# Attention block of a transformer layer on 8 cores: the first key, query, value and output-weight loads issued from the value-transpose stage instead of the attention stage

## What is computed

```python
x = x + attn(layernorm(x), Wq, Wk, Wv, Wo)
x = x + ffn(layernorm(x), W0, bias0, W1, bias1)   # 2048 -> 8192 -> 2048, gelu

def attn(x, Wq, Wk, Wv, Wo):
    q, k, v = x @ Wq.T, x @ Wk.T, x @ Wv.T         # split in 16 heads
    q, k = rope(q), rope(k)
    kw, vw = [previous block, own block] of k, v   # blocks of 512 rows
    scores = q @ kw.T / sqrt(128), masked to j > i and j <= i + 512
    return (softmax(scores) @ vw) @ Wo.T
```

## Time and profile before

| what | us |
|---|---|
| the two timed executions | 3869.8 and 4254.2 |
| their median | 4062.0 |
| the profiled execution's own time | 3853.5 |
| its span (first to last instruction, core 7) | 3851.9 |
| spans of the 8 cores | 3837.4 to 3851.9 |
| mean granted TensorE clock of the cores | 0.937 to 0.943 of full |

### The profile page before, as it was taken

One profiled execution on the slowest core, in us unless ns is written; L12 is line 12 of the kernel. 1 busy time (PEld: TensorE's weight loads), 2 busy tenths in 40 slices (PEclk: granted clock), 3 DMA queues, 4 the chain that ended last, 5 costly groups with the idle time before them and its releaser, 6 DMA issues. The chain is left out here.

```text
span 3851.9 us, 47166 instructions; the slowest of 8 cores (3837.4 to 3851.9 us)
## 1 busy us (share of the span) xinstructions
PE 3273.1 (85%) x17600; PEld 1632.0 (42%) x17600; DVE 785.8 (20%) x1618; ACT 786.3 (20%) x1285; POOL 592.9 (15%) x933
## 2 busy tenths in 40 slices
PE   1599999997357576676749999999997999999999
PEld 1344444443244453535434444444443444444444
DVE  5555554000034444434320000000000000000000
ACT  3355554111332332414101111111110000000000
POOL 1000101001300000000010000001203433443321
PEclk9999999999589888888959999999998999999999
DMA  9322555542774224060262333332807989899764
GB/s 239 100 62 62 99 103 102 100 96 71 256 138 146 74 75 145 1 218 2 82 162 69 82 82 82 82 82 58 150 39 184 225 209 221 212 223 224 198 196 124
DMA packets 191858, 488.96 MB, mean 127 GB/s; under 512 B 21776, under 2 KB 54544, under 8 KB 188816
## 3 DMA queue, kind: packets, MB, share of 16 engines
q0 software_dynamic: 132304, 304.97, 37.6%
q1 hardware_dynamic: 59328, 180.97, 14.2%
HBM read 487.96 MB, written 115.34 MB: 157 GB/s over the span
## 5 line engine op out<-in xcount | busy, mean ns | idle before, releaser
L1186 PE MATMUL pool<-w1q,gq 128*128 128x512 bf16 x4096 | 899.4, 380 | 35.2 <-DMA gq<-g_sp 35.2
L1041 PE MATMUL pool<-ln2T,w0b 128*128 128x512 bf16 x4096 | 886.4, 380 | 2.0 <-PEq L120 2.0
L370 PE MATMUL pool<-ln1T,wbuf 128*128 128x512 bf16 x3584 | 777.0, 380 | 6.6 <-PE pool L370 4.6
L1186 PEld LDWEIGHTS pool<-w1q,gq 128*128 128x128 bf16 x4096 | 396.6, 98 | 521.7 <-issue 55.9
L1041 PEld LDWEIGHTS pool<-ln2T,w0b 128*128 128x128 bf16 x4096 | 401.2, 98 | 487.0 <-issue 5.3
L370 PEld LDWEIGHTS pool<-ln1T,wbuf 128*128 128x128 bf16 x3584 | 350.4, 98 | 433.0 <-issue 13.5
L144 DVE TENSOR_TENSOR obuf<-pool,yh 128x512 f32<-128x512 f32 x64 | 44.3, 691 | 1795.2 <-PE pool L1190 1695.7
L1117 POOL DMA_DIRECT2D gq<-g_sp x256 | 225.4, 900 | 749.1 <-PE pool L1190 558.4
L170 ACT ACTIVATE gst<-pool,bias_s 128x2048 bf16<-128x2048 f32 x64 | 125.9, 1967 | 745.1 <-PE pool L1041 745.1
L785 PE MATMUL pool<-wo_sb,outT 128*128 128x512 bf16 x1024 | 237.0, 394 | 33.3 <-DVE ybuf L889 29.3
L814 ACT ACTIVATE expb<-pool 128x640 bf16<-128x640 f32 x256 | 180.1, 705 | 277.9 <-PE pool L728 271.9
(11 more groups left out here) (59 smaller groups left out, 1927.5 us busy)
## 6 DMA issues: line engine op xcount, KB each, us to landing
gq<-g_sp POOLq DMA_DIRECT2D x256, 512.0 KB, 12.1
w0b<-w_t POOLq DMA_DIRECT2D x128, 256.0 KB, 16.3
g_sp<-gst SPq DMA_DIRECT2D x64, 512.0 KB, 2.6
w1q<-w_t POOLq DMA_DIRECT2D x256, 128.0 KB, 19.3
xb<-x_ctx SPq DMA_DIRECT2D x20, 1024.0 KB, 11.1
wbuf<-wk_t POOLq DMA_DIRECT2D x64, 256.0 KB, 15.1
wbuf<-wv_t POOLq DMA_DIRECT2D x64, 256.0 KB, 14.9
xh<-x_ctx SPq DMA_DIRECT2D x32, 512.0 KB, 5.7
```

The lines of the kernel that those rows point to most:

```text
L370: ins = tn.matmul(pool[:, slot * 2048 + k * 512: slot * 2048 + (k + 1) * 512], lhs, ln1T[:, roff: roff + 512], start=(i == 0), stop=(i == ...
L1041: ins = tn.matmul(pool[:, slot * 2048 + scv * 512: slot * 2048 + (scv + 1) * 512], lhs, ln2T[:, i * TOWN + scv * 512: i * TOWN + (scv + 1) ...
L1186: tn.matmul(pp, lhs, w1q[hq4 % 2][:, n * 512: (n + 1) * 512], start=(n == 0), stop=False)
```

## The change

The five tensors kring, vring, qring, wo_sb and msk get their SBUF space before the value-transpose stage and keep it through the attention stage. The first query block's loads of k and q, the mask and the output weights are issued from within the value-transpose stage, behind the second group of vtl loads; the first loads of v follow behind the fifth group, after a wait for the first 8 tiles of v_sp (4 on each of SP's two write semaphores). In the attention stage POOL's first work is the loads of query block 1. Within a query block the order is now k, q, v (before: k, v, q). Nothing else is changed.

```diff
+        def ring_kq(g, qb):
+            for o0 in range(0, 16, 4):
+                g.dma_start(
+                    kring[:, o0 * 1024:(o0 + 4) * 1024].rearrange(
+                        "p (o c) -> p o c", c=1024),
+                    k_spv[:, o0: o0 + 4, qb * 512: qb * 512 + 1024]
+                ).then_inc(sem["sRing"], 16)
+            for o0 in range(0, 16, 8):
+                g.dma_start(
+                    qring[:, o0 * 512:(o0 + 8) * 512].rearrange(
+                        "p (o c) -> p o c", c=512),
+                    q_spv[:, o0: o0 + 8, qb * 512:(qb + 1) * 512]
+                ).then_inc(sem["sRing"], 16)
+
+        def ring_v(g, qb):
+            for j0 in range(0, 8, 2):
+                g.dma_start(
+                    vring[:, j0 * 2048:(j0 + 2) * 2048].rearrange(
+                        "p (j f) -> p j f", f=2048),
+                    v_spv[:, qb * 4 + j0: qb * 4 + j0 + 2, :]
+                ).then_inc(sem["sRing"], 16)
+
+        def wo_msk_load(g):
+            g.dma_start(msk[:], msk_in).then_inc(sem["sMsk"], 16)
+            for i0 in range(0, 16, 4):
+                g.dma_start(
+                    wo_sb[:, i0 * 2048:(i0 + 4) * 2048].rearrange(
+                        "p (i f) -> p i f", f=2048),
+                    wo_tv[:, i0: i0 + 4, :]
+                ).then_inc(sem["sWo2"], 16)
+
...
                                     vT_sp[o * 128:(o + 1) * 128,
                                           sg4 * 512:(sg4 + 1) * 512]
                                 ).then_inc(vs, 16)
+                            if sg4 == 1:
+                                wo_msk_load(g)
+                                ring_kq(g, 0)
+                        g.wait_ge(sem["sSpVa"], 16 * 4)
+                        g.wait_ge(sem["sSpVb"], 16 * 4)
+                        ring_v(g, 0)
...
                 def _(g):
                     barrier(g)
-                    g.dma_start(msk[:], msk_in).then_inc(sem["sMsk"], 16)
...
-                    rings(0)
-                    for i0 in range(0, 16, 4):
-                        g.dma_start(
-                            wo_sb[:, i0 * 2048:(i0 + 4) * 2048].rearrange(
-                                "p (i f) -> p i f", f=2048),
-                            wo_tv[:, i0: i0 + 4, :]
-                        ).then_inc(sem["sWo2"], 16)
                     for qb in range(1, NQB):
                         g.wait_ge(sem["sQbPE"], qb)
-                        rings(qb)
+                        ring_kq(g, qb)
+                        ring_v(g, qb)
```

More of the change, by code:

```diff
@@ L503, in _ @@
                         s.wait_ge(sem["sSpQb"], 16 * (NP1_G // 2))
+        p2o = ExitStack()
+        kring = p2o.enter_context(nc.sbuf_tensor("kring", [128, 16 * 1024], BF16))
+        vring = p2o.enter_context(nc.sbuf_tensor("vring", [128, 8 * 2048], BF16))
+        qring = p2o.enter_context(nc.sbuf_tensor("qring", [128, 16 * 512], BF16))
+        wo_sb = p2o.enter_context(nc.sbuf_tensor("wo_sb", [128, 16 * 2048], BF16))
+        msk = p2o.enter_context(nc.sbuf_tensor("msk_s", [128, 5 * 640], BF16))
+        k_spv = k_sp.rearrange("(o p) t -> p o t", p=128)
+        v_spv = v_sp.rearrange("(s p) f -> p s f", p=128)
+        q_spv = q_sp.rearrange("(o p) t -> p o t", p=128)
+        wo_tv = wo_t.rearrange("(i p) f -> p i f", p=128)
+        def ring_kq(g, qb):
[26 more added lines that the diff above has]
+                ).then_inc(sem["sWo2"], 16)
         if DO_V:
@@ L585, in build_nc @@
         with p2:
[L586 to L590, removed]
             expb = [p2.enter_context(nc.sbuf_tensor(f"expb{j}", [128, 640], BF16))
@@ L658, in _ @@
                     barrier(g)
-                    g.dma_start(msk[:], msk_in).then_inc(sem["sMsk"], 16)
[L661 to L667, removed]
-                            g.dma_start(
[L669 to L685, removed]
-                    rings(0)
-                    for i0 in range(0, 16, 4):
-                        g.dma_start(
-                            wo_sb[:, i0 * 2048:(i0 + 4) * 2048].rearrange(
-                                "p (i f) -> p i f", f=2048),
-                            wo_tv[:, i0: i0 + 4, :]
-                        ).then_inc(sem["sWo2"], 16)
+                    if not DO_V:
+                        wo_msk_load(g)
+                        ring_kq(g, 0)
+                        ring_v(g, 0)
                     for qb in range(1, NQB):
                         g.wait_ge(sem["sQbPE"], qb)
-                        rings(qb)
+                        ring_kq(g, qb)
+                        ring_v(g, qb)
                 @blk.tensor
@@ L915, in _ @@
                             v.sig(sem["sNmr"])
+        p2o.close()
         if MAX_PHASE < 3:
```

## The result

The changed kernel is slower by 1.15%: the ratio to the kernel before is 1.0115, with a 95% interval of 1.0086 to 1.0145. On the 3870 us of the kernel before that is some +44 us (33 to 56). By a bound of 2% the two are the same. Forecast were +33 us, a ratio of 1.0086. The profiled execution took 3906.5 us, and the lowest of 11 timed ones 3900.6, against 3853.5 and 3845.1 of before. The median of all eleven, 4091.0, lies outside my range, since executions of both kernels fall in two groups several per cent apart, whatever the kernel, and the comparison uses the faster group alone.

A forecast was written before the change was run, and what follows sets the result against it. DMA, not TensorE, was taken to limit the value-transpose stage and first attention loads. Terms -41.7 (ring wait), +73 (eleven loads), +0 (rest of stage), +2 (v loads) gave +33 on 3853.5, or 3886.5 us; range 3862 to 3925.

The forecast's parts named there:

- the rest of the stage: Value transposes from tile 8 to the barrier: pace stays at 49 us, +0; bounds 25 us less, 23 us more.
- the eleven loads: Mask, output weights, k and q queued ahead of the third vtl group make tile 8 of the transposes later: +73 us.
- The ring wait that goes: Start of attention: k, q, v and mask land before the barrier, so TensorE's load wait disappears: -41.7 us.
- starved-writes rival: Value-transpose stage: SP's v_sp writes slow beside POOL's full queue; +64 us in all, 3917.5 us; chance 0.16.
- The v loads at the stage's end: vring's loads, issued after the wait for 8 v_sp tiles, land about at the barrier: +2 us remaining wait.
- Sum: Whole kernel: -41.7 + 73 + 2 = +33 us, giving 3886.5 us; chance 0.64.
- The base and the range: Whole kernel: counted from the profiled execution's 3853.5 us, with a range from 3862 to 3925 us.
- The second way: Before the first score: all DMA time needed, 158 us from about 946, ends at 1104, or +28 us.
- Clock: Transposes: clock at half before and after, and attention starts from there either way: 0 us.
- absorbed: Value-transpose stage: free DMA time takes the moved loads, stage keeps 89 us, ring wait goes; 3811.8 us; chance 0.08.
- Interleaved: Value-transpose stage: vtl loads served beside wo_sb, tile 8 under 73 us late, DMA total rules; +28, 3881.5 us; chance 0.12.
- an estimate of +11: Alternative sum from the skill's HBM share: wo_sb read as f32, some 50 MB, 140 us; set aside for the rows' rates.

The follow-up runs named there:

- e2_wo_only: Changed kernel with only mask and output weights moved early; first k, q and v loads back behind the barrier; profiled execution 3899.4 us, no ratio taken.
- e1: Changed kernel with the four output-weight loads last in POOL's queue of the value-transpose stage, behind the v loads; ratio 1.0117 to the kernel before.
- e3: Changed kernel with the output weights behind the fifth vtl group, ahead of the v loads; profiled execution 3941.6 us, no ratio taken.
- e4: Changed kernel with all moved loads behind the fifth vtl group, in the order mask, k, q, v, output weights; ratio 1.0089 to the kernel before.
- e6_late_wo_after: As e4, but the output weights are issued behind the barrier, as before the change; ratio 0.9973 to the kernel before.
- e8: As e4, but two of the four output-weight loads are issued behind the barrier; profiled execution 3927.5 us, no ratio taken.

## Why the prediction was right and where it was wrong

The mechanism was right: the moved output weights hold up the third vtl group. Two steps failed. The sum came out 8 us too small, for the most part by the +0 for the rest of the stage (measured +5.4) and by +73 for the eleven loads (+76.8). And the range of the total time left no room for how far single executions lie apart. By step:

- *The ring wait that goes, -41.7:* right. It is 42.2 by the medians (1032.9 to 1075.1) and under 1 us after.
- *Eleven loads ahead of the third vtl group, +73:* right in mechanism and nearly in size. Tile 8 is late by 76.8 us (985.3 to 1062.1). Its parts stand up on their own: without the output weights tile 8 came at 1010 (1007 worked out), with them alone at 1043 (1038), and undoing their part gave back 51.7 us where 50.8 were charged.
- *The rest of the stage, +0:* this is the term of the sum that failed most. From tile 8 to the barrier it takes 53.0 us instead of 47.6, +5.4. I had written that the pace stays. From tile 8 on, SP's writes land in 5.6 us where they took 3.1, and ScalarE waits for them 24.5 us instead of 19.3 (medians over the cores). Of the 51.1 and 30.3 us that it waits in the whole stage, the larger part of the difference lies ahead of tile 8, where TensorE waited for the third group anyway. So a part of the starved-writes rival was real, 5 of its 23 us. That the loads queued beside the writes are the cause is supported by the other orders: from tile 8 to the last transpose it takes 46 to 57 us in all the kernels that have more than vtl loads queued there, 40.4 before, and 33.5 in e2_wo_only, where the writes land in 2.8 us. No run changed the queue and nothing else.
- *The v loads at the stage's end, +2:* nothing. On core 4 they were in by 1103.2, ahead of the barrier at 1113.9.
- *Sum:* -42 + 77 + 5 + 0 = +40, where I had +33. The interval of the ratio, 33 to 56, has my value at its edge.
- *The base and the range:* I counted from one profiled execution, 3853.5, and put only half of its distance of 16 us to the lower timed one into the range. That holds for executions like it: the profiled one took 3906.5. But the two timed ones of the kernel before lay 384 us apart, I had seen that, and gave the range no room for it. The median of all timed ones is 4091.0, 166 us above the range's end of 3925. What the runs show instead is a spread of 3900.6 to 4391.6, as wide as that of the kernel before, 3845.1 to 4335.4.
- *The second way, all DMA time together:* it gave 1104, or +28, and was the more general one. Four orders of the same loads (the changed kernel, e1, e3, e4) have their first score within 1.4 us of each other, at 1115 to 1116. Its reason was incomplete: I took it that nobody waits for the output weights once they are issued late enough. By my own steps e4_all_late should have won 14 us, and it lost 41. The wait at the block's end for POOL's loads wasn't in my account at all. In the changed kernel it costs nothing: on core 4 POOL's drain ends at 1105.8, and SP's wait for its last write only at 1113.5.
- *Clock, 0:* not as I wrote. On core 4 the granted clock is 0.87 from 1061 to 1075, right behind the long wait, so mostly at the upper of its two levels, and 0.50, the lower one, from there to 1113; the 16 transposes of a tile take 1.05 us at the one and 1.86 at the other. It shows in no mark, since ScalarE and the writes set the pace.
- *Two small slips:* in slice 11 the DMA digit is 7, not 7 to 9, and the eleven issues add up to 8.3 us in the rows, not 8.4. Nothing hangs on either.
- *The rivals:* absorbed was wrong, since the stage grew by 79 us. Interleaved was wrong too. SP's writes starving was right to a quarter. The HBM share of about 358 GB/s that the Trainium skill states ("DMA: Bandwidth & Descriptors", section "Where 436 GB/s comes from") gave an estimate of +11, where +41 was measured. The trace's own rates were the better guide.

## What to carry to other kernels

Before a load is issued earlier, ask what is free there in DMA time, not in engine time: this stage had TensorE idle for more than half, and 22 us of DMA time free for 91 us of loads. On one queue a load that nobody waits for goes behind all that somebody waits for. And where blocks end in a barrier, put it on the far side of the barrier if it may run on, for a block here did not end before POOL's loads had landed.

## What the runs showed of the hardware that I had not expected

POOL's drain at the end of a block did not end before POOL's last load had landed, though it waits for no semaphore. In each of the ten kernels it ended the same time behind that landing on all 8 cores, to within 0.01 us. From kernel to kernel this time goes from 1.2 us (e6_late_wo_after) to 3.5 (e2_wo_only); it is 1.3 in e4_all_late, 2.6 in the changed kernel and 3.3 in the kernel before. Why it differs stays open. Where the drain ended last of all (e1, e3, e4, e6, e8), the barrier followed it by 0.5 us, so that it came 1.6 to 3.0 us behind the landing. It moved with that landing by 12 to 13 us per 2 MB load of output weights. In the kernel before the drain was over at 1018.4 on core 7, 15 us ahead of SP's wait, and could not be seen in the time.

SP's own drain took 0.01 us in every kernel, but the code has SP wait for all its writes by semaphore ahead of it. Whether SP's hardware queue would be held in the same way wasn't tried.
